# Routed adapter with LayerNorm on one core: who makes the low halves of the weights, and the order of the first tiles

## The chip, the cores and the metric

One NeuronCore of a Trainium2 chip. The metric is the device time of the kernel in microseconds. The engines are named as in the profile: PE (TensorE), DVE (VectorE), ACT (ScalarE), POOL (GpSimd), SP (SyncE, which here only issues DMAs).

## What is computed

Each of 64 batches of 64 rows of 512 numbers goes through one of three experts, chosen by an integer per batch.

```python
Wd = W_down[stream]; bd = b_down[stream]      # 512 x 256, 256
Wu = W_up[stream];   bu = b_up[stream]        # 256 x 512, 512
g = ln_w[stream];    b = ln_b[stream]
h = jnp.einsum('bsh,bhk->bsk', x, Wd) + bd[:, None, :]
h = jax.nn.gelu(h, approximate=False)
h = jnp.einsum('bsk,bkh->bsh', h, Wu) + bu[:, None, :]
h = x + h
mean = jnp.mean(h, axis=-1, keepdims=True)
var = jnp.mean(jnp.square(h - mean), axis=-1, keepdims=True)
h = (h - mean) * jax.lax.rsqrt(var + 1e-05)
return h * g[:, None, :] + b[:, None, :]
```

## The kernel before, in words

The batches are sorted by expert on the chip, so that two batches of the same expert share a tile of 128 rows; there are 33 tiles. Float32 products are made of three matmuls in a rounded format: a number is its high half (a cast on ACT) plus its low half (the difference to the cast), and a product is high by high, high by low, low by high. So each weight and each activation has a `_hi` and a `_lo` tile.

One tile t goes through these steps, each a helper in the code:

- PE `transpose_x` (L843) turns x into PSUM; ACT `x_hi` (L436) and DVE `x_lo` (L659) make its two halves; PE `down` (L850) is 12 matmuls with W_down.
- DVE `down_bias` (L665) adds the bias, ACT `gelu` (L441), PE `transpose_g` (L866), ACT `g_hi` (L446), DVE `g_lo` (L673).
- POOL `add_bias` (L358) adds x and b_up into `xb`; ACT `seed` (L451) copies that into the PSUM bank in which PE `up` (L873) then adds six matmuls with W_up.
- DVE `stats` (L679), `mean_var` (L684) and `variance` (L688); POOL `power` (L367) makes rstd; DVE `scale` (L694) makes `scaled`, ACT `rescale` (L458) makes `normed`, POOL `shift` (L373) makes `res`, which SP stores for one half of the rows and ACT for the other.

Every engine does its instructions in the order in which they are written, and waits by semaphores. In the steady loop PE does for tile t: `transpose_g(t)`, `down(t+1)`, `transpose_x(t+3)`, `up(t)`. The first tiles ("the head") are written out by hand on every engine: ACT from L488 to L535, DVE from L722 to L758, PE from L899 to L927, POOL from L384 to L399. The parts of the head that matter here:

- POOL first makes the sums of tiles 0 to 2, then the low half of W_up's second part (`w_up_low`, L255), the sum of tile 3, the low half of the third part, and then for t from 0: `shift(t-1)`, `power(t)`, `add_bias(t+4)`. DVE makes the low half of the first part, at L728.
- `rescale(t)` waits for `shift(t-2)`, because `normed` has two buffers (PAR); `scaled` has four (DEEP).
- `up(0)`, `up(1)` and `up(2)` each wait for the low half of the part of W_up that the tile needs.
- The tail of the sort (four small instructions on one partition, L653 to L657) is on DVE. It makes the places of the stores.
- SP issues the loads in the order: x0, x1, W_up part 0, x2, W_up part 1, x3, x4, W_up part 2, x5, ln_w, x6, ln_b, x7 and on.
- PE fills its waits at the start with `warm_up` matmuls on a tile of ones; `WARM_UPS` (L59) has their numbers.

## Time and profile before

| | us |
|---|---|
| median of 3 runs | 145.44 (144.79 to 146.06) |
| the profiled execution | 146.48 |
| its span | 144.3 |
| PE busy in the span | 130.2 (90%) |
| DVE busy | 111.7 (77%) |
| POOL busy | 106.4 (74%) |
| ACT busy | 85.7 (59%) |

The span is from the first to the last instruction of the program; the rest of the execution's time (2.2 us) lies around it. PEclk is the granted clock of TensorE as a share of 2.4 GHz; its lower level is half of that. PE's busy time counts matmuls; weight loads (PEld) overlap them. An entry such as "[0.82 <-POOL xb L364]" says how long the engine had been idle and what released it.

### The profile page before, as it was taken

The page shows a single profiled execution, that of the slowest core. Times are in us where ns is not written, and L with a number is a line of the kernel's source. Part 1 is how long each engine was busy: PE and PEld are TensorE (multiplying, and loading weights), DVE is VectorE, ACT ScalarE, POOL GpSimd, SP SyncE. Part 2 cuts the span into 40 slices and gives each one's busy share as a digit, 9 for nine tenths or more (in the row PEclk, how much of TensorE's full clock was granted, in tenths as well). Part 3 has the DMA queues.
Part 4 walks back from the last instruction along what each step waited for, and adds up shares of the span by engine and source line. Part 5 has one row for each costly group of instructions (what it writes and reads, how often), then busy time and mean ns, then how long its engine had stood idle before and what let it go on. Part 6 is the DMA issues. An engine that isn't in the chain of part 4 may idle for free.

```text
span 144.3 us, 4085 instructions
## 1 busy us (share of the span) xinstructions
PE 130.2 (90%) x850; PEld 116.8 (81%) x851; DVE 111.7 (77%) x275; ACT 85.7 (59%) x177; POOL 106.4 (74%) x113
## 2 busy tenths in 40 slices
PE   6899896899619999999999999999999999999840
PEld 6799795789518999999999999999999899998620
DVE  1896954869427588978897988888888888888993
ACT  1675749526446466657766666666666667666710
POOL 6000696925598388889889888998898889988961
PEclk9999999999975899999999999999999999999999
DMA  2959899844214434455444555545555653332366
GB/s 53 350 164 259 286 322 319 236 145 137 57 35 133 119 103 145 145 148 148 145 145 148 145 145 148 145 145 145 147 165 148 173 130 73 77 79 45 74 168 184
DMA packets 13200, 21.94 MB, mean 152 GB/s; under 512 B 2297, under 2 KB 3842, under 8 KB 13186
## 3 DMA queue, kind: packets, MB, share of 16 engines
q1 hardware_dynamic: 8802, 15.74, 36.1%
q10 hardware_dynamic: 4384, 6.05, 15.7%
q8 instruction: 4, 0.07, 0.2%
q14 instruction: 10, 0.08, 0.2%
HBM read 13.39 MB, written 8.65 MB: 153 GB/s over the span
## 4 chain that ended last, share of the span: by engine, by line
PE 62%; POOL 4%; DVE 3%; issue 1%; ACT 1%; POOLq 1%; ACTq 1%; DVEq 0%
PE hg_ps L861 25%; PE y_ps L894 25%; PE xT_ps L847 7%; PE hg_ps L870 4%; POOL res L381 2%; DVE res L718 1%; POOL rstd L370 1%; POOL xb L364 1%; DVE y_ps L709 1%; POOLq L208 1%; ACT normed L464 0%; DVE r_stats L682 0%; ACTq L433 0%; DVE hb L670 0%; ACT y_ps L456 0%
## 5 line engine op out<-in xcount | busy, mean ns | idle before, releaser
L381 POOL TENSOR_TENSOR res<-normed,lnb_rows 128x512 f32<-128x512 f32 x31 | 39.9, 1287 | 18.4 <-ACT normed L464 18.3
L364 POOL TENSOR_TENSOR xb<-x_sb,bu_rows 128x512 f32<-128x512 f32 x33 | 43.7, 1326 | 12.6 <-ACT bu_rows L486 12.6
L444 ACT ACTIVATE g<-hb 128x256 f32<-128x256 f32 x33 | 13.8, 418 | 35.8 <-DVE hb L670 35.7
L894 PE MATMUL y_ps<-wu_hi,gT_hi 128*128 x66 | 23.9, 444 | 6.3 <-ACT gT_hi L449 5.1
L682 DVE BATCH_NORM_STATS2 r_stats<-y_ps 128x6 f32<-128x512 f32 x33 | 23.0, 697 | 8.2 <-issue 4.4
L861 PE MATMUL hg_ps<-wd_hi,xT_hi 128*128 x132 | 24.3, 307 | 0.0
L464 ACT ACTIVATE normed<-scaled,rstd 128x512 f32<-128x512 f32 x31 | 22.4, 724 | 2.4 <-issue 2.4
L662 DVE TENSOR_TENSOR xT_lo<-xT_ps,xT_hi 128x512 fp32r<-128x512 f32 x33 | 22.7, 689 | 1.0 <-ACT xT_hi L439 1.0
L703 DVE SCALAR_TENSOR_TENSOR scaled<-y_ps,r_mv,lnw_rows 128x512 f32<-128x512 f32 x31 | 22.9, 743 | 0.0
L894 PE MATMUL y_ps<-wu_lo,gT_hi 128*128 x66 | 21.1, 402 | 0.5 <-POOL wu_lo L258 0.5
L861 PE MATMUL hg_ps<-wd_lo,xT_hi 128*128 x132 | 21.4, 285 | 0.0
L861 PE MATMUL hg_ps<-wd_hi,xT_lo 128*128 x132 | 21.3, 283 | 0.0
L894 PE MATMUL y_ps<-wu_hi,gT_lo 128*128 x66 | 21.1, 402 | 0.0
L456 ACT COPY y_ps<-xb 128x512 f32<-128x512 f32 x33 | 19.5, 590 | 2.1 <-POOL xb L364 2.0
L670 DVE TENSOR_TENSOR hb<-hg_ps,bd_rows 128x256 f32<-128x256 f32 x33 | 14.0, 423 | 7.8 <-PE hg_ps L861 7.2
L439 ACT CAST xT_hi<-xT_ps 128x512 fp32r<-128x512 f32 x33 | 18.9, 572 | 1.7 <-PE xT_ps L847 1.7
L676 DVE TENSOR_TENSOR gT_lo<-hg_ps,gT_hi 128x256 fp32r<-128x256 f32 x33 | 13.8, 418 | 7.8 <-ACT gT_hi L449 7.5
L847 PE MATMUL xT_ps<-ident,x_sb 128*128 128x128 f32 x132 | 19.6, 272 | 0.0
L370 POOL TENSOR_TENSOR rstd<-var_eps,half_neg 128x1 f32<-128x1 f32 x33 | 18.3, 553 | 1.4 <-DVE var_eps L691 1.4
L861 PEld LDWEIGHTS hg_ps<-wd_hi,xT_hi 128*128 128x128 f32 x132 | 18.3, 194 | 0.3 <-issue 0.2
L861 PEld LDWEIGHTS hg_ps<-wd_hi,xT_lo 128*128 128x128 f32 x132 | 18.3, 192 | 0.0
L861 PEld LDWEIGHTS hg_ps<-wd_lo,xT_hi 128*128 128x128 f32 x132 | 18.3, 192 | 0.0
(87 smaller groups left out, 157.0 us busy)
## 6 DMA issues: line engine op xcount, KB each, us to landing
x_sb<-in_x_dram SPq DMA_DIRECT2D x64, 128.0 KB, 2.8
out_dram<-res ACTq DMA_DIRECT2D x33, 128.0 KB, 2.4
out_dram<-res SPq DMA_DIRECT2D x33, 128.0 KB, 2.3
wd<-in_L_cond_W_down_dram ACTq DMA_DIRECT2D x3, 512.0 KB, 4.9
wu<-in_L_cond_W_up_dram SPq DMA_DIRECT2D x3, 512.0 KB, 4.8
lnw_rows<-in_L_cond_ln_w_dram SPq DMA_DIRECT2D x1, 768.0 KB, 6.3
lnb_rows<-in_L_cond_ln_b_dram SPq DMA_DIRECT2D x1, 768.0 KB, 8.0
x_sb<-in_x_dram ACTq DMA_DIRECT2D x2, 128.0 KB, 2.8
```

What stands on the lines that cost most here:

```text
L364: pool.tensor_tensor(xb[:, c % DEEP, :], x_sb[:, c % FAR, :], bu_rows[:, ds(e * H, H)], ALU.add).then_inc(xb_ready, 1)
L370: pool.tensor_tensor(rstd[:, c % DEEP:c % DEEP + 1], var_eps[:, c % DEEP:c % DEEP + 1], half_neg[:], ALU.pow).then_inc(rstd_ready, 1)
L381: pool.tensor_tensor(res[:, c % FAR, :], normed[:, c % PAR, :], lnb_rows[:, ds(e * H, H)], ALU.add).then_inc(res_ready, 1)
L439: act.copy(xT_hi[:, c % PAR, :], xT_ps[c % PAR][:]).then_inc(xhi_ready, 1)
L456: act.copy(y_ps[c % YBANKS][:], xb[:, c % DEEP, :]).then_inc(seeded, 1)
L464: act.activation(normed[:, c % PAR, :], scaled[:, c % DEEP, :], ACT.Copy, scale=rstd[:, c % DEEP:c % DEEP + 1]).then_inc(normed_ready, 1)
L662: dve.tensor_tensor(xT_lo[:, c % PAR, :], xT_ps[c % PAR][:], xT_hi[:, c % PAR, :].bitcast(F32), ALU.subtract).then_inc(xlo_ready, 1)
L682: dve.bn_stats(r_stats[:, c % DEEP, :], y_ps[c % YBANKS][:]).then_inc(stats_ready, 1)
L703: dve.scalar_tensor_tensor(out=scaled[:, c % DEEP, :], in0=y_ps[c % YBANKS][:], scalar=r_mv[:, c % DEEP, 0:1], in1=lnw_rows[:, ds(e * H, H ...
L847: mm = pe.transpose(xT_ps[c % PAR][:, k * P:(k + 1) * P], x_sb[:, c % FAR, k * P:(k + 1) * P], ident[:])
L861: mm = pe.matmul(h, x_half[:, c % PAR, k * P:(k + 1) * P], w_half[:, ds(w0 + k * BN, BN)], start=(w_half is wd_hi and x_half is xT_hi and ...
L894: mm = pe.matmul(y_ps[c % YBANKS][:], g_half[:, c % PAR, k * P:(k + 1) * P], w_half[:, ds(w0 + k * H, H)], start=False, stop=(n == 2 and k ...
```

## The change

What it does:

- DVE makes the low halves of all three parts of W_up, the first behind `down_bias(1)`, the second behind `stats(0)`, the third behind `stats(1)`. POOL makes none; it goes on with sums. `up(1)` and `up(2)` do their low-half matmuls last (high by high, low by high, high by low).
- `normed` gets four buffers: `rescale(t)` waits for `shift(t-4)`.
- The tail of the sort moves from DVE to POOL, as five small steps and a copy, each with a wait on the one before.
- POOL's head is written out: `power` and `add_bias` of three tiles come before the first `shift`.
- ACT, DVE and PE get new hand-written heads; the copies of bu into SBUF come earlier; W_up's third part is loaded before x4; one of the banks in which the down bias is spread changes; `WARM_UPS` is 10, 4, 3, 2.

```diff
-    WARM_UPS = 9, 4, 4, 2
+    WARM_UPS = 10, 4, 3, 2
-        normed = sb("normed", [P, PAR, H])
+        normed = sb("normed", [P, DEEP, H])
-        bd_banks = [y_ps[E][:], hg_ps[0][:, 0:E * BN - H]]
+        bd_banks = [y_ps[E][:], hg_ps[1][:, H - BN:H]]
...
@@ SP
             load_w_up(sp, 1, from_expert[1])
-            for t in range(3, 5):
+            load(3, 3, entries(3, 0, 2))
+            load_w_up(sp, 2, from_expert[2])
+            for t in range(4, 6):
                 load(t, t, entries(t, 0, 2))
-            load_w_up(sp, 2, from_expert[2])
-            load(5, 5, entries(5, 0, 2))
@@ POOL
-            pool.wait_ge(slots_ready, 2)
+            def mark(ins, steps):
+                ins.then_inc(marking, 1)
+                pool.wait_ge(marking, steps)
+            pool.wait_ge(rows_ready, 2)
+            pool.tensor_copy(slot_batch_f[:], slot_batch[:]).then_inc(marking, 1)
+            mark(pool.tensor_tensor(slot_step[:], key_f[:, 1:1 + SLOTS], key_f[:, 0:SLOTS], ALU.subtract), 2)
+            mark(pool.tensor_scalar(slot_same[:], slot_step[:], 0.0, float(B), ALU.is_equal, ALU.mult), 3)
+            mark(pool.tensor_tensor(slot_step[:], slot_same[:], slot_batch_f[:], ALU.add), 4)
+            mark(pool.tensor_copy(slot_store[:], slot_step[:]), 5)
+            pool.tensor_copy(io_table[:].rearrange("p (t n) -> p t n", n=3)[:, STORE_A_LAG:, 2],
+                             slot_store[:, 0:SLOTS:2]).then_inc(slots_ready, 1)
...
             for t in range(3):
                 add_bias(t, t)
-            w_up_low(pool, 1).then_inc(wu_lo_rest, 1)
             add_bias(3, 3)
-            w_up_low(pool, 2).then_inc(wu_lo_rest, 1)
+            for t in range(3):
+                power(t, t)
+                add_bias(t + DEEP, t + DEEP)
+            shift(0, 0)
+            power(3, 3)
+            shift(1, 1)
+            add_bias(3 + DEEP, 3 + DEEP)
+            power(4, 4)
+            shift(2, 2)
+            add_bias(4 + DEEP, 4 + DEEP)
+            shift(3, 3)
             def body(t, c):
-                if exists(t - 1):
-                    shift(t - 1, c - 1)
+                shift(t - 1, c - 1)
                 power(t, c)
                 add_bias(t + DEEP, c + DEEP)
-            for t in range(FAR + 1):
+            for t in range(5, FAR + 1):
                 body(t, t)
@@ ACT
-                if from_tile(t, PAR):
-                    act.wait_ge(res_ready, t - PAR + 1)
-                act.activation(normed[:, c % PAR, :], scaled[:, c % DEEP, :], ACT.Copy,
+                if from_tile(t, DEEP):
+                    act.wait_ge(res_ready, t - DEEP + 1)
+                act.activation(normed[:, c % DEEP, :], scaled[:, c % DEEP, :], ACT.Copy,
...
             wd_high(2)
+            for e in range(E - 1):
+                keep_up_bias(e)
+            x_hi(0, 0)
+            x_hi(1, 1)
             for part in range(len(bd_banks)):
                 keep_down_bias(part)
-            x_hi(0, 0)
-            keep_up_bias(0)
-            x_hi(1, 1)
-            keep_up_bias(1)
+            seed(0, 0)
             wu_high(0)
             gelu(0, 0)
-            seed(0, 0)
             g_hi(0, 0)
             x_hi(2, 2)
+            gelu(1, 1)
             wu_high(1)
-            gelu(1, 1)
+            seed(1, 1)
             g_hi(1, 1)
+            gelu(2, 2)
             x_hi(3, 3)
-            seed(1, 1)
-            gelu(2, 2)
+            wu_high(2)
+            g_hi(2, 2)
+            seed(2, 2)
+            gelu(3, 3)
             x_hi(4, 4)
-            seed(2, 2)
-            wu_high(2)
-            g_hi(2, 2)
-            gelu(3, 3)
-            x_hi(5, 5)
             seed(3, 3)
             g_hi(3, 3)
             gelu(4, 4)
+            x_hi(5, 5)
             x_hi(6, 6)
             seed(4, 4)
             rescale(0, 0)
@@ DVE
-            link(dve.tensor_copy(slot_batch_f[:], slot_batch[:]))
...
+            dve.wait_ge(up_spread, E)
+            dve.tensor_copy(bu_rows[:, (E - 1) * H:E * H], y_ps[E - 1][:]).then_inc(bu_last_ready, 1)
...
             x_lo(0, 0)
-            dve.wait_ge(up_spread, E)
-            dve.tensor_copy(bu_rows[:, (E - 1) * H:E * H], y_ps[E - 1][:]).then_inc(bu_last_ready, 1)
             x_lo(1, 1)
             dve.wait_ge(bd_ready, len(bd_banks))
             down_bias(0, 0)
-            w_up_low(dve, 0).then_inc(wu_lo_first, 1)
+            down_bias(1, 1)
+            w_up_low(dve, 0).then_inc(wu_lo_ready, 1)
             g_lo(0, 0)
-            down_bias(1, 1)
             x_lo(2, 2)
             stats(0, 0)
+            dve.wait_ge(stats_ready, 1)
+            w_up_low(dve, 1).then_inc(wu_lo_ready, 1)
+            down_bias(2, 2)
             g_lo(1, 1)
-            dve.wait_ge(stats_ready, 1)
-            down_bias(2, 2)
             mean_var(0, 0)
             variance(0, 0)
             x_lo(3, 3)
             stats(1, 1)
+            dve.wait_ge(stats_ready, 2)
+            w_up_low(dve, 2).then_inc(wu_lo_ready, 1)
             g_lo(2, 2)
-            dve.wait_ge(stats_ready, 2)
+            mean_var(1, 1)
             down_bias(3, 3)
-            mean_var(1, 1)
             variance(1, 1)
...
             x_lo(5, 5)
             scale(1, 1)
+            stats(3, 3)
+            g_lo(4, 4)
+            dve.wait_ge(stats_ready, 4)
+            down_bias(5, 5)
+            mean_var(3, 3)
+            variance(3, 3)
+            x_lo(6, 6)
             scale(2, 2)
+            scale(3, 3)
@@ PE
+                parts = [(gT_hi, wu_hi), (gT_lo, wu_hi), (gT_hi, wu_lo)] if early else [
+                    (gT_hi, wu_hi), (gT_hi, wu_lo), (gT_lo, wu_hi)]
...
-            pe.wait_ge(bd_ready, len(bd_banks))
             down(0, 0, expert_of(pe, 0))
             e0, e1 = experts_from(0)
+            pe.wait_ge(bd_ready, len(bd_banks))
             down(1, 1, e1)
             transpose_g(0, 0)
             transpose_x(2, 2)
             up(0, 0, e0)
-            transpose_x(3, 3)
...
             down(2, 2, e_down)
             transpose_g(1, 1)
-            transpose_x(4, 4)
+            transpose_x(3, 3)
             up(1, 1, e_up)
-            body(2, 2)
-            tiles(pe, body, 3, TILES - 4)
+            transpose_g(2, 2)
+            down(3, 3, e_down)
+            transpose_x(4, 4)
+            up(2, 2, e_up)
+            transpose_g(3, 3)
+            down(4, 4, e_down)
+            transpose_x(5, 5)
+            transpose_x(6, 6)
+            up(3, 3, e_up)
+            tiles(pe, body, 4, TILES - 4)
```

## Rows read from the trace of the kernel before

**Rows 1.** Page of the profile, TensorE's granted clock in 40 equal slices of the span, in tenths

```profile
PEclk9999999999975899999999999999999999999999
```

**Rows 2.** Table by stretch; columns: stretch, length, busy time (count) by engine, PEclk, DMA share, GB/s

```profile
18.00:23.40 5.40, 4.18 (x28) 3.64 (x28) 3.21 (x10) 3.24 (x7) 5.40 (x4) 1.00 0.97 328
42.60:48.60 6.00, 5.95 (x24) 5.26 (x25) 3.35 (x9) 2.37 (x5) 5.09 (x6) 0.54 0.43 133
48.60:131.80 83.20, 83.20 (x576) 75.70 (x575) 71.99 (x168) 55.83 (x120) 71.49 (x70) 1.00 0.47 133
```

**Rows 3.** Chain that ended last; columns: start us, us, engine, tile, line

```profile
39.77 0.55 POOL rstd L370
40.32 1.24 POOL xb L364
...
48.86 1.40 PE y_ps L894 x6
...
50.47 1.43 PE hg_ps L861 x12
51.90 0.44 PE xT_ps L847 x4
52.33 1.40 PE y_ps L894 x6
```

**Rows 4.** Timeline, ScalarE; columns: start us, us, engine, line, operation, tiles, [idle before]

```profile
37.13 0.59 ACT L456 COPY y_ps<-xb 128x512 f32<-128x512 f32 x1 [0.82 <-POOL xb L364]
37.66 0.72 ACT L464 ACTIVATE normed<-scaled,rstd 128x512 f32<-128x512 f32 x1
40.74 0.72 ACT L464 ACTIVATE normed<-scaled,rstd 128x512 f32<-128x512 f32 x1 [2.36 <-issue]
...
42.15 0.36 ACT L449 CAST gT_hi<-hg_ps 128x256 fp32r<-128x256 f32 x1
```

**Rows 5.** Timeline, GpSimd, in the head

```profile
15.72 1.28 POOL L364 TENSOR_TENSOR xb<-x_sb,bu_rows 128x512 f32<-128x512 f32 x1 [12.56 <-ACT bu_rows L486]
...
16.96 2.28 POOL L364 TENSOR_TENSOR xb<-x_sb,bu_rows 128x512 f32<-128x512 f32 x1
...
25.61 2.39 POOL L258 TENSOR_TENSOR wu_lo<-wu,wu_hi 128x1024 fp32r<-128x1024 f32 x1 [1.56 <-ACT wu_hi L469]
...
34.05 1.28 POOL L381 TENSOR_TENSOR res<-normed,lnb_rows 128x512 f32<-128x512 f32 x1 [4.28 <-ACT normed L464]
```

**Rows 6.** Timeline, TensorE, in the head

```profile
18.07 0.73 PE L894 MATMUL y_ps<-wu_hi,gT_hi 128*128 x2 [0.47 <-ACT gT_hi L449]
...
23.45 0.73 PE L894 MATMUL y_ps<-wu_hi,gT_hi 128*128 x2 [1.21 <-ACT y_ps L456]
...
42.65 1.22 PE L894 MATMUL y_ps<-wu_hi,gT_hi 128*128 x2 [4.10 <-ACT gT_hi L449]
...
48.61 0.71 PE L894 MATMUL y_ps<-wu_hi,gT_hi 128*128 x2
```

**Rows 7.** Timeline, VectorE, in the head

```profile
7.51 1.21 DVE L252 TENSOR_TENSOR wd_lo<-wd,wd_hi 128x1024 fp32r<-128x1024 f32 x1
...
15.85 2.24 DVE L258 TENSOR_TENSOR wu_lo<-wu,wu_hi 128x1024 fp32r<-128x1024 f32 x1
```

**Rows 8.** Page, costliest groups: busy us, mean ns of one, idle before and its releaser

```profile
L444 ACT ACTIVATE g<-hb 128x256 f32<-128x256 f32 x33 | 13.8, 418 | 35.8 <-DVE hb L670 35.7
...
L682 DVE BATCH_NORM_STATS2 r_stats<-y_ps 128x6 f32<-128x512 f32 x33 | 23.0, 697 | 8.2 <-issue 4.4
...
L662 DVE TENSOR_TENSOR xT_lo<-xT_ps,xT_hi 128x512 fp32r<-128x512 f32 x33 | 22.7, 689 | 1.0 <-ACT xT_hi L439 1.0
...
L670 DVE TENSOR_TENSOR hb<-hg_ps,bd_rows 128x256 f32<-128x256 f32 x33 | 14.0, 423 | 7.8 <-PE hg_ps L861 7.2
L439 ACT CAST xT_hi<-xT_ps 128x512 fp32r<-128x512 f32 x33 | 18.9, 572 | 1.7 <-PE xT_ps L847 1.7
```

**Rows 9.** DMA issues from 16.4 to 17.5 us; last column: us to landing

```profile
wu<-in_L_cond_W_up_dram SPq DMA_DIRECT2D x1, 512.0 KB, 5.5
```

More of the change, by code:

```diff
@@ L120, in adapter_program @@
         slot_same = sb("slot_same", [1, SLOTS])
+        slot_step = sb("slot_step", [1, SLOTS])
         slot_store = sb("slot_store", [1, SLOTS], I32)
@@ L172, in adapter_program @@
         wd_lo_ready = sem("wd_lo_ready")
-        wu_lo_first = sem("wu_lo_first")
-        wu_lo_rest = sem("wu_lo_rest")
+        wu_lo_ready = sem("wu_lo_ready")
+        rows_ready = sem("rows_ready")
+        marking = sem("marking")
         bu_last_ready = sem("bu_last_ready")
@@ L380, in shift @@
                     pool.wait_ge(stored[c % FAR], landed_count(t - FAR, c))
-                pool.tensor_tensor(res[:, c % FAR, :], normed[:, c % PAR, :], lnb_rows[:, ds(e * H, H)],
+                pool.tensor_tensor(res[:, c % FAR, :], normed[:, c % DEEP, :], lnb_rows[:, ds(e * H, H)],
                                    ALU.add).then_inc(res_ready, 1)
@@ L645, in _ @@
             w_down_low(dve, 0).then_inc(wd_lo_ready, 1)
-            dve.tensor_copy(key_f[:], key_filled[:])
-            link(dve.tensor_scalar(slot_batch[:], key_filled[:, 1:1 + SLOTS], B - 1, None, ALU.bitwise_and))
+            dve.tensor_copy(key_f[:], key_filled[:]).then_inc(rows_ready, 1)
+            dve.tensor_scalar(slot_batch[:], key_filled[:, 1:1 + SLOTS], B - 1, None, ALU.bitwise_and).then_inc(
+                rows_ready, 1)
             dve.wait_ge(wd_hi_ready, 2)
@@ L651, in _ @@
             w_down_low(dve, 2).then_inc(wd_lo_ready, 1)
-            link(dve.tensor_copy(slot_batch_f[:], slot_batch[:]))
-            link(dve.tensor_tensor(slot_same[:], key_f[:, 1:1 + SLOTS], key_f[:, 0:SLOTS], ALU.is_equal))
-            link(dve.scalar_tensor_tensor(out=slot_store[:], in0=slot_same[:], scalar=float(B), in1=slot_batch_f[:],
-                                     op0=ALU.mult, op1=ALU.add))
-            dve.tensor_copy(io_view[:, STORE_A_LAG:, 2], slot_store[:, 0:SLOTS:2]).then_inc(slots_ready, 1)
+            dve.wait_ge(up_spread, E)
+            dve.tensor_copy(bu_rows[:, (E - 1) * H:E * H], y_ps[E - 1][:]).then_inc(bu_last_ready, 1)
             def x_lo(t, c):
@@ L779, in body @@
                 return near[3], near[2]
-            for t in range(4, 6):
-                body(t, t % UNROLL)
+            body(5, 5)
             tiles(dve, body, 6, TILES - 3)
@@ L875, in up @@
                 w0 = e * (KB * H)
+                early = isinstance(t, int) and 0 < t < E
                 pe.wait_ge(ghi_ready, t + 1)
-                if isinstance(t, int) and t == 0:
-                    pe.wait_ge(wu_hi_ready, 1)
-                if isinstance(t, int) and t == 1:
-                    pe.wait_ge(wu_hi_ready, 2)
-                if isinstance(t, int) and t == 2:
-                    pe.wait_ge(wu_hi_ready, 3)
-                pe.wait_ge(seeded, t + 1)
-                for n, (g_half, w_half) in enumerate(((gT_hi, wu_hi), (gT_hi, wu_lo), (gT_lo, wu_hi))):
-                    if isinstance(t, int) and t == 0 and n == 1:
-                        pe.wait_ge(wu_lo_first, 1)
-                    if isinstance(t, int) and t == 1 and n == 1:
-                        pe.wait_ge(wu_lo_rest, 1)
-                    if isinstance(t, int) and t == 2 and n == 1:
-                        pe.wait_ge(wu_lo_rest, 2)
+                if isinstance(t, int) and t < E:
+                    pe.wait_ge(wu_hi_ready, t + 1)
+                pe.wait_ge(seeded, t + 1)
+                parts = [(gT_hi, wu_hi), (gT_lo, wu_hi), (gT_hi, wu_lo)] if early else [
+                    (gT_hi, wu_hi), (gT_hi, wu_lo), (gT_lo, wu_hi)]
+                for n, (g_half, w_half) in enumerate(parts):
+                    if w_half is wu_lo and isinstance(t, int) and t == 0:
+                        pe.wait_ge(wu_lo_ready, 1)
+                    if w_half is wu_lo and isinstance(t, int) and t == 1:
+                        pe.wait_ge(wu_lo_ready, 2)
+                    if w_half is wu_lo and isinstance(t, int) and t == 2:
+                        pe.wait_ge(wu_lo_ready, 3)
                     if g_half is gT_lo:
@@ L901, in _ @@
             transpose_x(1, 1)
-            warm_up(WARM_UPS[3], hg_ps[1])
+            warm_up(WARM_UPS[3], hg_ps[0])
             pe.wait_ge(wd_hi_ready, E)
-            pe.wait_ge(bd_ready, len(bd_banks))
             down(0, 0, expert_of(pe, 0))
             e0, e1 = experts_from(0)
+            pe.wait_ge(bd_ready, len(bd_banks))
             down(1, 1, e1)
@@ L924, in _ @@
             transpose_g(1, 1)
[L925 to L928 removed]
+            transpose_x(3, 3)
+            up(1, 1, e_up)
+            e_up, e_down = experts_from(2)
+            transpose_g(2, 2)
+            down(3, 3, e_down)
+            transpose_x(4, 4)
+            up(2, 2, e_up)
+            e_up, e_down = experts_from(3)
+            transpose_g(3, 3)
[4 more added lines that the diff above has]
+            tiles(pe, body, 4, TILES - 4)
             body(TILES - 3, TILES - 3)
```

3 lines of the change are left out of this document (1 added, 2 removed).

## The prediction, made before the changed kernel was run

> **What bounds the kernel now.** I read the page first, for the row of TensorE's granted clock: it is full in every slice but three or four, near a third of the span [rows 1]. Something stops PE once. The table by stretch then says what PE does elsewhere: from 48.6 to 131.8 us it is busy for 83.20 of 83.20 us at the full clock, while from 42.6 to 48.6 it is just as busy at 0.54 of it, and from 18.0 to 23.4 it is busy for 4.18 of 5.40 us at 1.00 [rows 2]. So the steady part is bound by PE alone and nothing on another engine can shorten it; what can be won lies before 48.6 us. In the chain of waits a steady tile is four pieces of PE: six matmuls of `up` 1.40, `transpose_g` about 0.2, `down` 1.43, `transpose_x` 0.44, and the start of `up` comes again after 52.33 - 48.86 = 3.47 us [rows 3]. I call 3.48 a tile.
>
> The same chain, just ahead of the steady part, is on POOL: a `power` of 0.55 us, then a sum of 1.24 us [rows 3]. The timeline of ACT says why that matters: `seed(5)` came after 0.82 us of idling for POOL's sum, `rescale(1)` after it, `rescale(2)` only after 2.36 us of idling, and `g_hi(5)` at 42.15 behind that and behind `seed(6)` [rows 4]. The reader should see one queue catching another: POOL idles 4.28 us in front of `shift(0)` until ACT has done `rescale(0)` [rows 5]; `power(1)`, the sum of tile 5, `shift(1)`, `power(2)` and the sum of tile 6 are all queued behind that one wait; and ACT's next steps, `g_hi(5)` among them, are queued behind these. PE has idled 4.10 us when `up(5)` begins at 42.65, and `up(6)` begins at 48.61, 5.96 us later where a tile takes 3.48: the low clock costs 2.5 us on top [rows 6]. From `up(0)` at 18.07 to `up(6)` at 48.61 it is 30.5 us for six tiles, whose work is 6 x 3.48 = 20.9. The 9.7 us between are: the stop before `up(5)` 4.1 + the low clock 2.5, the stop of 1.21 before `up(1)` [rows 6], and some 1.9 in small pieces, POOL's two late low halves of 2.39 us among them [rows 5].
>
> **The change, part by part.** The sum is made up to the start of `up(6)`, behind which PE is full either way.
>
> *POOL's head.* Three powers and the sums up to tile 6 now stand before the first `shift`. They wait for `variance` on DVE and for free buffers of `xb`, not for a `rescale`. `power(2)` needs `variance(2)`, which follows `stats(2)` after `up(2)`; by the walk below it is there at 31.0 and the sum of tile 6 at about 32.5, and ACT wants them at about 36. The cover is 3 us or more, and without it ACT would pay what is missing one for one. What is removed is the stop before `up(5)` and, if PE has no other long stop, the low clock behind it: up to 6.6 us.
>
> *Low halves.* Two POOL instructions of 2.39 us [rows 5] go and DVE gets two more. The price on DVE has two rows: 1.21 for the same shape in W_down's case, 2.24 for the first part of W_up, which ran while POOL made sums; the second of these sums took 2.28 where its neighbour took 1.28 [rows 5, 7]. So a low half costs 1.21 alone and 2.24 beside a sum, and a sum next to it 1.28 or 2.28. I take 1.21 for the first two, because POOL has no sum to do then (it has done those of tiles 0 to 2, and waits for x3 or for `variance(0)`), and 1.5 for the third, which meets the sum of tile 4. If all three cost 2.24, each puts about 1.0 us into its `up`: 3 us in all.
> The Trainium skill (SBUF — State Buffer, section "SBUF: two separate sides") says that a VectorE instruction with two SBUF inputs and a GpSimd instruction that reads SBUF exclude each other for the whole instruction, the later one waiting for the other's end. By that rule the 2.24 is 1.03 of waiting and 1.21 of work, and the price depends on where POOL is when it starts, not on being beside it; the trace agrees: 15.72 + 1.28 = 17.00, and 17.00 + 1.1 is 18.09, where the DVE instruction ended. The sum by the rule is the one with 1.21, 1.21 and 1.5; by a plain reading of the row it is the one with three times 2.24, the second rival below.
>
> *Tail of the sort.* Four instructions on one partition leave DVE at a place where it then waits for `x_hi(0)`: nothing gained. On POOL six small ones with a wait each come where it idles 12.56 us for the bias rows [rows 5]. Their inputs are there near 9.0, right behind the first W_down low half, which ends at 7.51 + 1.21 = 8.7 [rows 7]. No row shows such a step; the nearest is a `power`, 0.55 [rows 3], on 128 partitions. From below nothing, from above 0.55 and as much again for its wait, six times, 6.6 us: done between 9.0 and 15.6. I take the half, 12.3. The bias rows are then ready too, so the first sum starts near 13, before its 15.72 of now; at the upper end it starts where it does now and `up(0)` loses the 0.6 that I give it below. Value 0, range 0 to 0.6.
>
> *Walk through the head.* Durations: `gelu` 0.42, `stats` 0.70, `x_lo` 0.69, `down_bias` and `g_lo` (same size) 0.42, `x_hi` 0.57 [rows 8]; a third of `up` 0.47; a chained instruction on ACT starts 0.06 to 0.1 before the end of the one before it [rows 4]. `seed(0)` no longer stands between `transpose_g(0)` and `g_hi(0)`, which gives back its 0.59: `up(0)` starts at 17.5, not 18.07. But the low half of part 0 now stands behind `down_bias(1)`, which ends about 17.2; it ends at 18.4, so `up(0)` holds for 0.5 us after its first third and is done at 19.4. `down(2)` to 20.85, `transpose_g(1)`, `g_hi(1)`: `up(1)` at 21.6 against 23.45 [rows 6], since the 1.21 us for `seed(1)` are gone. DVE: `stats(0)` 19.65 to 20.35, low half of part 1 to 21.55, `down_bias(2)`, `g_lo(1)` to 22.4; `up(1)` holds 0.3 and ends 23.35. `down(3)` and `transpose_x(4)` take it to `up(2)` at 25.4. DVE: `stats(1)` to 24.2, low half of part 2 to 25.7, `g_lo(2)` 26.1; `up(2)` holds 0.3, ends 27.1. `down_bias(3)` ends 26.7, `gelu(3)` 27.15, `x_hi(4)` 27.65: `down(4)` starts 27.7, 0.4 us of holding. It and two `transpose_x` bring `up(3)` to 30.0, and without a stop `up(4)` comes at 33.5. Then ACT's own queue: `gelu(5)` ends about 34.3, and `x_hi(7)`, `seed(5)`, `rescale(1)`, `rescale(2)`, `seed(6)`, `g_hi(5)` stand one behind the other, 0.57 + 0.59 + 0.72 + 0.72 + 0.59 + 0.36 less six overlaps of 0.08 = 3.1 [rows 4, 8]: `up(5)` at 37.5, 0.5 after PE is free. `up(6)` at 41.0.
> So 48.61 - 41.0 = 7.6 us. The walk leaves out small delays of each release, and in such walks these only add; I take 7.4. The longest hold in it is 0.5 us, shorter than the 1.21 that left the clock at full [rows 2, 6].
>
> *Loads.* W_up's third part goes ahead of x4. It was issued at 16.5 and took 5.5 us to land, so 22.0, at a time when the DMA engines are 0.97 busy [rows 2, 9]; ahead of x4's two transfers it is there by about 21, wanted by ACT at 22.8. x4 lands later by one 512 KB transfer, 512 KB at 328 GB/s = 1.6 us [rows 2], about 21.2, wanted at 23.1 by the sum and at 24.9 by PE. Both hidden by some 2 us; the cost if that is gone is the lateness itself.
>
> *Rest.* Four buffers of `normed`: in the steady part PE is full, so nothing. One more `warm_up` at the start and one less later lie where PE waits for the sort or for x0: 0, at most 0.3 either way. The other bank for the down bias: 0. The end of the kernel keeps its order and its phase against PE: 0.
>
> Against the profiled execution: 146.48 - 7.4 = 139.1, with the 2.2 us around the span unchanged. The median of the runs shown is 1.0 below that execution; I take the same difference off it: 145.44 - 7.4 = 138.0.
>
> **The rivals.**
> 1. *The stop moves to tiles 7 to 9.* The sums of tiles 7 and 8 now stand behind `shift(1)` and `shift(2)`. ACT wants the sum of tile 9 before `g_hi(8)`, by 47.4; POOL has it, after `shift(3)`, `shift(4)` and `power(5)` at 1.28, 1.28 and 0.55 [rows 3, 5], at about 46.5. The reserve is under 1 us, and POOL is busy 71.49 of 83.20 us in the steady part [rows 2], so it catches up slowly. One tile's POOL work late is 1.28 + 0.55 + 1.24 = 3.1 us given back: 141.1; with the low clock 2.5 more, 143.6. For it: POOL was the cause before. Against: the reserve of 3 us at tiles 5 and 6.
> 2. *The shared port.* Each low half costs 2.24 and each displaced sum 2.28: 3 us of holding in `up(0)`, `up(1)`, `up(2)`, of which 0.3 is in the sum already: 138.0 + 2.7 = 140.7. For it: the one row of this kind [rows 7]. Against: POOL's idle time there.
> 3. *Slower: the clock falls in the head.* PE now holds inside `up(0)`, `up(1)`, `up(2)` and before `down(4)`, in a stretch where it is not full. If these holds bring the clock to the lower level at `up(0)`, each tile at that level costs 2.5 us more [rows 6]; it decides from three tiles on (7.5 us), and for the four up to `up(4)` the time is 138.0 + 10 = 148.0. For it: the only fall in the trace came where PE stopped, and PE's share is then below one. Against: at 4.18 busy of 5.40, with a stop of 1.21 in it, the clock stayed full [rows 2, 6], and my walk has a denser head than that.
> 4. *It does not do what it says.* `g_hi(5)` stays behind two `rescale`s and two `seed`s on ACT; if that queue and not POOL's was what held `up(5)`, only the small stops go, 1.5 to 2.5 us: 143.4. Against: ACT idled 0.82 and 2.36 us within it [rows 4].
>
> **How the numbers follow.** Forecast 0.66, rival 1 0.14, rival 2 0.09, rival 3 0.04, rival 4 0.07. The forecast's own range is 136.8 to 139.6: the walk's holds are 2.0 us in all, of which a half could be absent, and a sort's tail or a load could cost 0.5 to 1.5. Downward the end is PE without any hold, 7.4 + 2.0 = 9.4 saved, 136.0. For 8 in 10 I take half of rivals 1 and 2 in: 136.6 to 141.1. A difference under about 1% can't be told from none here, that is 1.45 us. Faster by over 1% (below 143.99): forecast, rivals 1 and 2 and most of 4, 0.92; within 1%: 0.04; slower: 0.04.
>
> **What would show it.** Right: PEclk full in all slices behind the start; `up(5)` with under 1.5 us of idle time before it; `up(6)` at 40.5 to 42; the two L258 instructions near 1.2 us and the third up to 2.4; no wait of POOL for `normed` in front of a sum before tile 7; the stretch from `up(6)` to the end as long as before. Wrong: a second dip of PEclk; ACT idling before `seed(8)` or `seed(9)` (rival 1); all three low halves at 2.2 (rival 2); PE idling before `up(5)` with ACT busy all through (rival 4).

## The result, and the profile after

The changed kernel takes 139.2 us in the median (138.98 to 139.67, 4 runs) against 145.22 for the kernel before on the same chip (144.79 to 146.06, 4 runs). The ratio is 0.9583, with a 95% interval of 0.9531 to 0.9634: 6.0 us less. The profiled execution took 139.21 us with a span of 137.2, against 146.48 and 144.3. A run more than 1.5% above the fastest of its kernel is left out of the ratios.

The page, PE's busy time and the granted clock in 40 slices:

```profile
PE 126.6 (92%) x850; PEld 112.5 (82%) x851; DVE 112.9 (82%) x273; ACT 85.1 (62%) x177; POOL 104.5 (76%) x117
...
PEclk9999999999999999999999999999999999999995
```

The dip of [rows 1] near a third of the span is gone, and PE is busy for 126.6 us where it was for 130.2: the same matmuls, none of them at the low clock behind a stop. The table by stretch, to lay beside [rows 2] (columns as there):

```profile
18.00:23.40 5.40, 5.29 (x30) 3.84 (x29) 4.58 (x10) 3.54 (x8) 1.92 (x3) 1.00 1.05 270
41.00:124.00 83.00, 83.00 (x574) 75.64 (x573) 71.81 (x169) 55.35 (x120) 73.02 (x72) 1.00 0.48 137
```

From 18.0 to 23.4 us PE is busy for 5.29 us instead of 4.18, and from 41 us on it is full, as it was from 48.6. The timeline of PE, the first matmuls of each `up` (and the second third of `up(0)`); the columns are start, duration, engine, line, operation, tiles, and in brackets the idle time before and who ended it:

```profile
17.51 0.73 PE L923 MATMUL y_ps<-wu_hi,gT_hi 128*128 x2
18.24 0.70 PE L923 MATMUL y_ps<-wu_lo,gT_hi 128*128 x2
...
21.85 0.73 PE L923 MATMUL y_ps<-wu_hi,gT_hi 128*128 x2
...
25.50 0.71 PE L923 MATMUL y_ps<-wu_hi,gT_hi 128*128 x2
...
29.85 0.71 PE L923 MATMUL y_ps<-wu_hi,gT_hi 128*128 x2
...
33.41 0.71 PE L923 MATMUL y_ps<-wu_hi,gT_hi 128*128 x2
...
37.74 0.73 PE L923 MATMUL y_ps<-wu_hi,gT_hi 128*128 x2 [0.60 <-ACT gT_hi L473]
...
41.23 0.71 PE L923 MATMUL y_ps<-wu_hi,gT_hi 128*128 x2
```

`up(5)` waits 0.60 us for `g_hi(5)` where it waited 4.10 [rows 6], and `up(6)` starts at 41.23 instead of 48.61. That is 7.4 us; the span is 7.1 us shorter, so the rest is 0.3 us longer. PE is full up to 124 us; about half of the 0.3 us is spread over the tiles (23 of them take 80.04 us, 79.89 before), the other half lies in the last tiles, where PE is no longer full. Its cause was not followed. ACT in front of `up(5)`, to lay beside [rows 4]:

```profile
34.96 0.59 ACT L480 COPY y_ps<-xb 128x512 f32<-128x512 f32 x1
35.48 1.34 ACT L488 ACTIVATE normed<-scaled,rstd 128x512 f32<-128x512 f32 x2
...
36.72 0.58 ACT L480 COPY y_ps<-xb 128x512 f32<-128x512 f32 x1
37.23 0.37 ACT L473 CAST gT_hi<-hg_ps 128x256 fp32r<-128x256 f32 x1
```

`seed(5)`, both rescales and `seed(6)` run one behind the other with no idle time between, where ACT had waited 0.82 and 2.36 us for POOL. (The view names "issue" for the 2.36; the last thing that `rescale(2)` needs is POOL's `power(2)`, which ended at 39.77 + 0.55 = 40.32 [rows 3], 0.42 us before it.) POOL in the head:

```profile
8.75 0.23 POOL L365 CAST slot_batch_f<-slot_batch 1x66 f32<-1x66 int32 x1 [5.60 <-DVE slot_batch L671]
8.96 1.26 POOL L366 TENSOR_TENSOR slot_step<-key_f 1x66 f32<-1x66 f32 x1
10.30 1.43 POOL L367 TENSOR_SCALAR slot_same<-slot_step 1x66 f32<-1x66 f32 x1
...
13.26 3.77 POOL L379 TENSOR_TENSOR xb<-x_sb,bu_rows 128x512 f32<-128x512 f32 x3 [0.54 <-issue]
19.38 1.29 POOL L379 TENSOR_TENSOR xb<-x_sb,bu_rows 128x512 f32<-128x512 f32 x1 [2.34 <-DMA x_sb<-in_x_dram]
...
33.09 1.28 POOL L396 TENSOR_TENSOR res<-normed,lnb_rows 128x512 f32<-128x512 f32 x1 [0.63 <-ACT normed L488]
```

Its first sum starts at 13.26 instead of 15.72, the three behind each other take 3.77 us with none stretched, and `shift(0)` at 33.09 waits for the same `normed` as before [rows 5], but nothing that ACT wants soon stands behind it. The first three lines of the fence are small steps of the sort, and two of them take 1.26 and 1.43 us on one partition; that comes back below. DVE's three low halves of W_up, to lay beside [rows 7]:

```profile
16.19 1.93 DVE L260 TENSOR_TENSOR wu_lo<-wu,wu_hi 128x1024 fp32r<-128x1024 f32 x1
...
20.18 1.56 DVE L260 TENSOR_TENSOR wu_lo<-wu,wu_hi 128x1024 fp32r<-128x1024 f32 x1
...
24.49 1.23 DVE L260 TENSOR_TENSOR wu_lo<-wu,wu_hi 128x1024 fp32r<-128x1024 f32 x1
```

### The profile page after: what moved, and what is told of

Read it like the earlier page. It is cut to its first block, busy times and chain, and to the rows that moved or that the text cites. A ratio compares the mean times of both kernels' runs of the same rounds, so it can differ in the third digit from the quotient of the medians.

```text
span 137.2 us, 4086 instructions
## 1 busy us (share of the span) xinstructions
PE 126.6 (92%) x850; PEld 112.5 (82%) x851; DVE 112.9 (82%) x273; ACT 85.1 (62%) x177; POOL 104.5 (76%) x117
## 4 chain that ended last, share of the span: by engine, by line
PE 70%; DVE 11%; POOL 6%; ACT 5%; issue 3%; DMA 2%; POOLq 1%; ACTq 1%; DVEq 0%
PE hg_ps L891 28%; PE y_ps L923 28%; PE xT_ps L877 8%; PE hg_ps L900 5%; POOL res L396 2%; DMA itok_all_i<-in_itok_B_dram 2%; DVE r_stats L704 1%; ACT xT_hi L463 1%; DVE hb L692 1%; ACT y_ps L480 1%; DVE res L740 1%; DVE scaled L725 1%; POOL slot_same L367 1%; POOL slot_step L366 1%; POOLq L210 1%
## 5 line engine op out<-in xcount | busy, mean ns | idle before, releaser
L379 POOL TENSOR_TENSOR xb<-x_sb,bu_rows 128x512 f32<-128x512 f32 x33 | 42.7, 1296 | 2.9 <-DMA x_sb<-in_x_dram 2.3
L923 PE MATMUL y_ps<-wu_hi,gT_hi 128*128 x66 | 23.3, 434 | 1.4 <-ACT gT_hi L473 1.2
L385 POOL TENSOR_TENSOR rstd<-var_eps,half_neg 128x1 f32<-128x1 f32 x33 | 18.2, 551 | 7.9 <-DVE var_eps L713 7.8
L923 PE MATMUL y_ps<-wu_lo,gT_hi 128*128 x66 | 20.6, 393 | 0.0
L877 PEld LDWEIGHTS xT_ps<-ident,x_sb 128*128 128x128 f32 x132 | 15.1, 140 | 0.8 <-DMA x_sb<-in_x_dram 0.5
```

What stands on the lines that cost most here:

```text
L379: pool.tensor_tensor(xb[:, c % DEEP, :], x_sb[:, c % FAR, :], bu_rows[:, ds(e * H, H)], ALU.add).then_inc(xb_ready, 1)
L385: pool.tensor_tensor(rstd[:, c % DEEP:c % DEEP + 1], var_eps[:, c % DEEP:c % DEEP + 1], half_neg[:], ALU.pow).then_inc(rstd_ready, 1)
L877: mm = pe.transpose(xT_ps[c % PAR][:, k * P:(k + 1) * P], x_sb[:, c % FAR, k * P:(k + 1) * P], ident[:])
L923: mm = pe.matmul(y_ps[c % YBANKS][:], g_half[:, c % PAR, k * P:(k + 1) * P], w_half[:, ds(w0 + k * H, H)], start=False, stop=(n == 2 and k ...
```

## The experiments

Two theories stood against each other. A: what cost the time was the order on POOL alone, a shift that waits with sums queued behind it. B: what cost it was POOL's load, the two low halves of 2.39 us [rows 5], with ACT's queue behind it. The kernel before ran beside every group of runs; its median was 145.76, 146.19, 145.56 and 144.95 us in the four groups, so kernels of different groups are compared by their ratios to it.

The record has the span of every run too. The device time lies 2.0 to 2.1 us above it in most runs, 1.7 to 1.8 in e4 and e5, and in some runs of several kernels 2.4 to 3.5; why is not known. With four runs of a kernel this can move a median by more than an edit does, so spans are given below where the two disagree. The changed kernel's are 136.9 to 137.6 us.

### One part alone, and that part taken out

`e1_sums_first` is the kernel before with one edit, `e2_shifts_first` the changed kernel with that edit undone.

```diff
-            def body(t, c):
-                if exists(t - 1):
-                    shift(t - 1, c - 1)
+            for t in range(3):
+                power(t, t)
+                add_bias(t + DEEP, t + DEEP)
+            shift(0, 0)
+            power(3, 3)
+            shift(1, 1)
+            add_bias(3 + DEEP, 3 + DEEP)
...
```

> The kernel before, with one edit: POOL's head in the new order (power and sum of tiles 0 to 2 ahead of the first shift). The low halves of W_up's parts 1 and 2 stay on POOL, the heads of ACT, DVE and PE stay as they were. Theory A (the shift that waits for rescale(0) holds up the sums queued behind it, and that is the stop before up(5)): the stop of 4.1 us shrinks to under 1 us, no low clock behind it, up(6) starts near 42.3 instead of 48.61, and the time is 139 to 140.5. Theory B (POOL is late because it also makes two low halves, and ACT's queue does the rest): the stop stays above 2.5 us and the time above 142.5.

> The changed kernel, with POOL's head put back into the old order (shift(t-1), power(t), sum t+4 from the start) and everything else of the change kept, the low halves on DVE and four buffers of normed among it. Theory A: the stop before up(5) is back with 4 us or more, with the low clock behind it, up(6) near 47.6, time 144.5 to 146: the rest of the change is worth almost nothing without the order. Theory B: POOL has no low halves any more, so the stop is under 2 us and the time 139.5 to 142.

e1: 139.7 us (139.25 to 140.23), ratio 0.9593 (0.9527 to 0.9659). e2: 145.73 us (144.43 to 146.96), ratio 1.0013 (0.9964 to 1.0062). PE's timeline of e1 at `up(5)` and `up(6)`:

```profile
39.05 0.72 PE L905 MATMUL y_ps<-wu_hi,gT_hi 128*128 x2 [0.45 <-ACT gT_hi L460]
...
42.54 0.71 PE L905 MATMUL y_ps<-wu_hi,gT_hi 128*128 x2
```

And of e2 the table by stretch, the stop before `up(5)` at 41.45 and what follows it:

```profile
41.00:46.50 5.50, 5.05 (x24) 4.50 (x25) 3.42 (x9) 2.69 (x7) 5.14 (x6) 0.69 0.49 143
36.90:41.45 4.55, 0.00 (x0) 0.00 (x1) 0.10 (x1) 1.89 (x4) 4.01 (x4) 1.00 0.22 59
```

With the order alone the stop is 0.45 us and `up(6)` starts at 42.54, where 42.3 was expected. Without it, all the rest of the change is worth nothing: PE does nothing at all for 4.55 us, and then works at 0.69 of its clock. Both halves of theory A hold. In e2 PE reaches the stop 1.7 us earlier than in the kernel before (`up(4)` starts at 33.17 against 34.83), and only stands longer for the same release.

### Who makes the low halves

`e3_lows_on_pool` is the changed kernel with the low halves of parts 1 and 2 back on POOL.

```diff
             for t in range(3):
                 add_bias(t, t)
+            w_up_low(pool, 1).then_inc(wu_lo_rest, 1)
             add_bias(3, 3)
+            w_up_low(pool, 2).then_inc(wu_lo_rest, 1)
...
-            w_up_low(dve, 1).then_inc(wu_lo_ready, 1)
-            w_up_low(dve, 2).then_inc(wu_lo_ready, 1)
```

> The changed kernel, with the low halves of parts 1 and 2 back on POOL at their old places (behind the sum of tile 2 and behind the sum of tile 3), the order of the rest kept. Theory A: no large stop; up(1) and up(2) wait for a low half of 2.39 us, which costs 0.5 to 1.5 us: 139.7 to 140.7. Theory B: the low halves are what made POOL late; the stop before up(5) returns with 2 us or more and the time is above 142.

138.82 us (138.68 to 139.63), ratio 0.9561 (0.9491 to 0.9631): below the 139.7 to 140.7 that my theory gave, and level with the changed kernel or a little below it (spans 136.6 to 136.8 us against 136.9 to 137.6). Theory B falls; so does my cost for the move.

```profile
17.58 0.73 PE L924 MATMUL y_ps<-wu_hi,gT_hi 128*128 x2
...
37.07 0.72 PE L924 MATMUL y_ps<-wu_hi,gT_hi 128*128 x2 [0.35 <-ACT gT_hi L476]
...
40.57 0.71 PE L924 MATMUL y_ps<-wu_hi,gT_hi 128*128 x2
```

From `up(0)` to `up(6)` it is 22.99 us here and 23.72 in the changed kernel. The likely reason, read from the queues and not tested apart: on DVE each low half stands in front of `down_bias` and `g_lo`, for which ACT and PE wait; on POOL, with the sums ahead, it stands in front of nothing that is wanted soon. The part of the change that its title names first gains nothing, and in this place may cost some tenths.

### The stop and the low clock, apart

`e4_stop_filled` and `e5_stop_filled` are the kernel before with PE kept at work during the stop, so that the clock stays. The first try:

```diff
+            pe.wait_ge(xlo_ready, 8)
+            warm_up(14, xT_ps[1])
             up(5, 5, e_up)
```

> The kernel before, with 14 warm_up matmuls on a bank that is free then, put before up(5), where PE stood still for 4.1 us; nothing is left out of the computation. It takes the low clock away and leaves the stop. If the low clock costs what the spacing of up(5) and up(6) says (2.5 us), up(6) starts 2.5 us earlier and the median is 142.5 to 143. Rival: the low clock costs the median nothing or under 1 us, since the runs of before that are not profiled may not have it: 144.3 or more.

150.23 us (148.82 to 150.59), ratio 1.0294 (1.0209 to 1.0380). PE's timeline:

```profile
44.97 4.84 PE L807 MATMUL xT_ps<-ones 128*128 128x128 f32 x28 [5.69 <-DVE xT_lo L663]
49.56 0.71 PE L895 MATMUL y_ps<-wu_hi,gT_hi 128*128 x2
```

I had overlooked that DVE makes `x_lo(7)` behind `g_lo(5)`, which waits for the same `g_hi(5)` as `up(5)`: the fill could only start when the stop was over, and ran in front of `up(5)`, its first 3 us at the low clock. It says nothing on the question. The second try uses the PSUM bank of tiles 3 and 7:

```diff
+            pe.wait_ge(scaled_ready, 4)
+            for _ in range(14):
+                mm = pe.matmul(y_ps[3][:, 0:P], ones[:], ones[:], start=False, stop=True, skip_group_check=True)
+            mm.then_inc(filled, 1)
             up(5, 5, e_up)
```

> The kernel before, with 14 matmuls on the ones tile put before up(5), on the PSUM bank of tiles 3 and 7, which is free from the end of scale(3) (seed(7) waits for the last of them); PE can start them where it stood still for 4.1 us. Nothing is left out of the computation. The stop stays, the low clock behind it goes: up(6) starts 3.5 us after up(5), the mean granted clock is 0.99 or more. If the low clock costs what the profiled execution shows (2.5 us), the median is 142.5 to 143.3. Rival: that execution had more of it than the others (mean clock 0.974; other executions of before have 0.973 to 0.986), and the median falls by only 1 to 2 us, 143.7 to 144.7.

143.33 us (143.21 to 143.64), ratio 0.9826 (0.9755 to 0.9897), mean granted clock 0.992 to 0.997.

```profile
38.09 3.29 PE L939 MATMUL y_ps<-ones 128*128 128x128 f32 x28
42.39 0.73 PE L898 MATMUL y_ps<-wu_hi,gT_hi 128*128 x2 [1.00 <-ACT gT_hi L451]
...
45.92 0.71 PE L898 MATMUL y_ps<-wu_hi,gT_hi 128*128 x2
```

`up(5)` starts at 42.39, where it was 42.65 before [rows 6], and `up(6)` 3.53 us behind it, where it took 5.96. So the low clock is worth 1.5 to 3.6 us by the ratio's interval, 2.5 in the middle; a gain there is beyond the noise, but whether it exceeds 2% is open. Of these 2.5 us some 0.3 lie outside the span (1.74 us there instead of 2.03). The order alone (e1) saves 5.9 us, so some 3.4 are left for the stop itself, which fits the 3.65 us by which it shrank (4.10 to 0.45). And the runs draw together: 0.4 us between the lowest and the highest, where the kernel before went from 144.76 to 146.42 in the six runs of the same group that the ratio uses. In the first group its thirteen runs have mean clocks of 0.973 to 0.986; at 0.975 and below their spans are 143.4 to 144.5 us, above that 142.5 to 143.4: how long the clock stays low differs from run to run. Two traces show it: in the kernel before it is at the lower level from about 41.3 to 48.1 us, in e2 from about 42.2 to 45.6, and `up(6)` follows `up(5)` by 5.96 and by 5.05 us.

### Two buffers of `normed`, and the sort's tail

`e7_two_normed` is the changed kernel with PAR for DEEP in `normed` and in the wait of `rescale`.

> The changed kernel, with two buffers of normed instead of four (rescale(t) waits for shift(t-2)). Theory: with the sums ahead of the shifts, each shift is done 1.5 us or more before the rescale that would wait for it (shift(0) ends at 34.4, rescale(2) starts at 36.1; shift(1) ends at 37.7, rescale(3) starts at 39.2), so nothing changes: 139.0 to 139.5, up(5) within 0.2 us of 37.74. Rival: two buffers bring the stop back in part, up(5) 1 us or more later, 140 or above.

139.32 us (139.06 to 140.23), ratio 0.9575 (0.9495 to 0.9655), `up(5)` at 37.53. The four buffers do nothing once the sums stand ahead.

`e6_tail_on_dve` is the changed kernel with the four instructions of the sort's tail back on DVE.

```diff
+            link(dve.tensor_copy(slot_batch_f[:], slot_batch[:]))
+            link(dve.tensor_tensor(slot_same[:], key_f[:, 1:1 + SLOTS], key_f[:, 0:SLOTS], ALU.is_equal))
...
             dve.wait_ge(up_spread, E)
```

> The changed kernel, with the four small instructions of the sort's tail back on DVE behind the third low half of W_down, and none on POOL. Theory: DVE copies the last bias rows about 0.9 us later, POOL's first sum starts at 13.9 to 14.2 instead of 13.26, seed(0), the first part's high half and gelu(0) follow by 0.5 us, up(0) starts near 18.0 instead of 17.51: 139.4 to 139.9. Rival: POOL's small steps of 1.26 and 1.43 us beside DVE's low halves go as well, nothing that PE waits for moves, 138.9 to 139.3.

139.68 us (139.53 to 140.43), ratio 0.9593 (0.9517 to 0.9670), `up(0)` at 17.94. `up(0)` is 0.43 us later, as the theory had it. The spans are 137.5 to 137.8 us against 136.9 to 137.6 of the changed kernel, and 137.0 to 137.5 of e7 beside it, so some 0.4 us; by the ratios it would be 0.15 us only, and their intervals overlap.

### The last hold, and what the rest of the head is worth

`e8_g_hi_first` is the changed kernel with this in ACT's head, and `body(6)` without its first two steps:

```diff
             seed(5, 5)
+            g_hi(5, 5)
             rescale(1, 1)
             rescale(2, 2)
+            seed(6, 6)
```

> The changed kernel, with g_hi(5) put ahead of rescale(1), rescale(2) and seed(6) in ACT's queue. Theory: the last hold in the head, 0.6 to 0.8 us before up(5) at 37.74, is ACT's own queue of 3.1 us behind gelu(5); it goes, up(5) starts near 36.95, up(6) near 40.4, and the time is 138.4 to 138.8. Rival: the rescales and the seed that are put back make tg(6) or up(6) late by as much, 139.0 to 139.5.

139.31 us (138.94 to 139.37), ratio 0.9555 (0.9486 to 0.9624).

```profile
17.96 0.73 PE L926 MATMUL y_ps<-wu_hi,gT_hi 128*128 x2
...
37.15 0.70 PE L926 MATMUL y_ps<-wu_hi,gT_hi 128*128 x2
...
40.62 0.70 PE L926 MATMUL y_ps<-wu_hi,gT_hi 128*128 x2
```

The hold before `up(5)` is gone: `up(0)` to `up(6)` is 22.66 us instead of 23.72. But `up(0)` itself came 0.45 us later than in the profile of the changed kernel, and the median stayed. The median hides the gain, though: the spans of the four runs are 136.9, 136.4, 136.4 and 136.6 us, against 136.9 to 137.6, some 0.6 us less, as the theory had it; the device times of the last three lie 2.7 to 3.0 us above their spans, those of the changed kernel 2.0 to 2.1. The rival, that something behind is late by as much, falls: `up(6)` follows `up(5)` by 3.47 us, and only `up(8)` comes 0.2 us late (3.68 behind `up(7)`). The profiled execution has the longest span of the four, and the question became what moves `up(0)`.

`e9_both` joins e3 and e8.

> The changed kernel with two edits: the low halves of W_up's parts 1 and 2 back on POOL (as in e3_lows_on_pool) and g_hi(5) ahead of the rescales (as in e8_g_hi_first). Theory: the low halves cost DVE more of the path than they cost POOL (up(6) came 22.99 us after up(0) in e3, 23.72 in the changed kernel), and the hold of 0.35 us before up(5) that was left in e3 goes too: up(6) 22.6 us after up(0), median 138.2 to 138.7, below the changed kernel and e3. Rival: POOL is late with two low halves, power(0) and the sums behind them hold up seed(5) or seed(6), and it is 138.9 or more.

138.59 us (138.27 to 139.36), ratio 0.9546 (0.9499 to 0.9594), `up(0)` at 17.94 and `up(6)` at 40.30, 22.36 us apart. The theory's number, with spans of 135.7 to 136.5 us.

### The port between DVE and POOL

`e10_sum_waits` is the changed kernel with one wait more on POOL.

```diff
-            for t in range(3):
+            for t in range(2):
                 add_bias(t, t)
+            pool.wait_ge(wu_lo_ready, 1)
+            add_bias(2, 2)
```

> The changed kernel; POOL's sum of tile 2 waits for DVE's first low half of W_up. Theory (exclusion: an instruction of DVE with two SBUF inputs waits for the end of the sum under way, and then works 1.09 us): the first low half takes 1.1 to 1.25 us instead of 1.93 and ends at 17.4, up(0) goes through without a hold of 0.25 us, and no sum is slowed; 138.8 to 139.2. Rival (the two share a port and slow each other in proportion, or the low half is slow for another reason, loads into SBUF for one): it still takes 1.6 us or more.

140.01 us (139.59 to 140.29), ratio 0.9638 (0.9577 to 0.9698). DVE's first low half of W_up:

```profile
16.87 1.22 DVE L260 TENSOR_TENSOR wu_lo<-wu,wu_hi 128x1024 fp32r<-128x1024 f32 x1 [0.50 <-ACT wu_hi L495]
```

It takes 1.22 us instead of 1.93, as exclusion has it, and `up(0)` goes through without a hold. The low half itself ended at 18.09, not at the 17.4 expected, because the high half that it needs came late. In the changed kernel the sum of tile 2 runs from 15.77 for 1.27 us, to 17.04, and the low half ends at 16.19 + 1.93 = 18.12, 1.08 us later; the next one ends at 21.74, 1.07 us behind the sum of tile 3 (19.38 + 1.29 = 20.67). The kernel was slower all the same, by 0.8 us of its ratio. For the profiled execution, whose span of 137.8 us is 0.6 above that of the changed kernel, POOL's timeline shows why:

```profile
9.33 2.30 POOL L365 CAST slot_batch_f<-slot_batch 1x66 f32<-1x66 int32 x1 [6.17 <-DVE slot_batch L673]
11.60 0.29 POOL L366 TENSOR_TENSOR slot_step<-key_f 1x66 f32<-1x66 f32 x1
```

The first of the sort's small steps, 0.23 us in the changed kernel's profile, takes 2.30 here. The data for it came at 9.3 us, just after DVE had begun two low halves of W_down one behind the other, 2.34 us from 9.19; the step ends when they end. In e9 it takes 1.17. POOL's first sum then starts at 13.96 instead of 13.26, and `seed(0)`, the high half of W_up's first part, `gelu(0)` and `up(0)` follow on ACT's queue in that order. So whether `up(0)` comes at 17.5 or at 18.2 hangs on a few tenths of a us near 9 us. The edit does not touch that stretch, so this delay is chance and not its price. The other three runs have spans of 137.0, 137.1 and 137.5 us, like the changed kernel's, and two of them carry 3.0 and 3.3 us outside the span: the edit has no clear cost or gain in the spans.

### Versions that are faster

`e11_low_first` is e9 with two pairs exchanged:

```diff
@@ ACT
-            seed(0, 0)
             wu_high(0)
+            seed(0, 0)
             gelu(0, 0)
@@ DVE
-            down_bias(1, 1)
             w_up_low(dve, 0).then_inc(wu_lo_ready, 1)
+            down_bias(1, 1)
```

> As e9_both, with the first low half of W_up ahead of down_bias(1) on DVE and the first high half ahead of seed(0) on ACT. Theory: the low half is there before up(0) needs it, so up(0)'s second third follows its first without the 0.25 us of holding, and down_bias(1) has 0.7 us to spare before gelu(1): 0.2 to 0.3 us below e9_both. Rival: the low half meets a sum there too, down_bias(1) and gelu(1) come late and up(1) with them, 0.3 us or more above e9_both.

137.67 us (137.25 to 138.97), ratio 0.9484 (0.9429 to 0.9539), 0.9 us below e9, more than the 0.2 to 0.3 expected. In e9 ACT waited for POOL's first sum, then made `seed(0)`, the high half of 1.04 us and `gelu(0)` (at 16.49); here it makes the high half while it would wait, from 13.93, and `gelu(0)` starts at 15.57:

```profile
17.02 0.73 PE L927 MATMUL y_ps<-wu_hi,gT_hi 128*128 x2
...
35.90 0.70 PE L927 MATMUL y_ps<-wu_hi,gT_hi 128*128 x2
...
39.37 0.70 PE L927 MATMUL y_ps<-wu_hi,gT_hi 128*128 x2
```

The low half did meet a sum, as the rival had it (2.31 us from 15.02), and `up(1)` still came 4.33 us behind `up(0)`; the time lost there was less than the time won.

`e12_tail_later` is e11 with the sort's tail moved on POOL:

```diff
-            pool.wait_ge(rows_ready, 2)
-            pool.tensor_copy(slot_batch_f[:], slot_batch[:]).then_inc(marking, 1)
...
-            for t in range(3):
+            for t in range(2):
                 power(t, t)
                 add_bias(t + DEEP, t + DEEP)
+            pool.wait_ge(rows_ready, 2)
+            pool.tensor_copy(slot_batch_f[:], slot_batch[:]).then_inc(marking, 1)
...
```

> As e11_low_first, with the six small steps of the sort's tail on POOL moved from ahead of its first sum to behind the sum of tile 5, where POOL idles some 2 us for variance(2). Theory: near 9 us these steps meet DVE's low halves of W_down, and the first of them takes 0.23 us or, where it comes just after a low half has begun, 1.17 (e9, e11) or 2.30 (e10); that sets when the first sum starts (13.26 to 13.96). Moved, each takes 0.45 or less, the first sum starts at 13.0 or before, the first low half of W_up ends earlier by the same, and the median is 137.1 to 137.6. Rival: the first sum has to wait for the bias rows until 13.5 anyway, or the moved steps hold up power(2), and the median is 137.7 or more.

137.19 us (137.12 to 138.44), ratio 0.9472 (0.9422 to 0.9521). POOL's timeline, the first sums and the first three moved steps, and PE's:

```profile
12.90 4.76 POOL L373 TENSOR_TENSOR xb<-x_sb,bu_rows 128x512 f32<-128x512 f32 x3 [9.74 <-DVE bu_rows L689]
...
28.50 0.23 POOL L405 CAST slot_batch_f<-slot_batch 1x66 f32<-1x66 int32 x1
28.69 0.29 POOL L406 TENSOR_TENSOR slot_step<-key_f 1x66 f32<-1x66 f32 x1
29.06 0.46 POOL L407 TENSOR_SCALAR slot_same<-slot_step 1x66 f32<-1x66 f32 x1
```

```profile
17.03 0.72 PE L931 MATMUL y_ps<-wu_hi,gT_hi 128*128 x2
...
38.90 0.71 PE L931 MATMUL y_ps<-wu_hi,gT_hi 128*128 x2
```

The first sum starts at 12.90, and beside no low half the steps take 0.23, 0.29 and 0.46 us. `up(6)` starts at 38.90, 2.3 us ahead of the changed kernel. This is the best version: 5.3% below the kernel before, where the change gives 4.2%. Against e11 it is a small step: spans of 135.1 to 135.3 us after 135.2 to 135.9, with ratios whose intervals overlap. The head still has 21.87 us for six tiles of 3.48.

## Why the prediction was right, and where it was off

**What bounds it, and the stop.** Right. PE is full behind the head in both kernels, the gain is the distance of the two `up(6)`, and the cause was the wait of `shift(0)` with the sums queued behind it: e1 has the gain with the order alone, e2 has none without it.

**The walk.** `up(0)` to `up(6)` were given as 17.5, 21.6, 25.4, 30.0, 33.5, 37.5 and 41.0; they came at 17.51, 21.85, 25.50, 29.85, 33.41, 37.74 and 41.23. ACT's queue behind `gelu(5)` was the last hold, 0.60 us for the 0.5 given, and e8 takes it away. Part of this closeness is luck: `up(0)` came at 17.51 here, but at 17.96 in e8 and 17.94 in e9, which are the same up to that point, and the first low half ended near the 18.4 of the walk (18.12) for another reason than the walk gave.

**Low halves.** The step that took 1.21 us for the first two, "because POOL has no sum to do then", was wrong: they took 1.93 and 1.56. DVE began the first at 16.19, not at 17.2, while the three sums, one behind the other from 13.26, ran until 17.04; and the sum of tile 3, which had waited 2.34 us for x3, ran until 20.67. The third, given 1.5, took 1.23. The second rival's 2.24 each was wrong as well: the price is what is left of the sum under way, and then 1.08. The Trainium skill's rule (SBUF — State Buffer, section "SBUF: two separate sides"), by which the later of the two waits for the end of the other's instruction, is borne out by these ends and by the 1.22 us of e10. What I did not see is that the move has no use at all: e3 is as fast without it.

**The sort's tail.** Given as done at 12.3 with a value of 0: it was done at 12.72. The value was 0.4 us (e6), on the side of a gain that I had excluded with the words "nothing gained"; DVE copies the last bias rows 0.9 us earlier, and in e6 POOL's first sum, and through it `up(0)`, waits for them. In the changed kernel the rows are there at 12.01, and the first sum (13.26) stands behind POOL's own last step of the sort (to 12.72) instead: e12, with the steps out of the way, has it at 12.90. That the small steps would meet DVE's low halves was not in my bounds by its cause; the upper bound of 6.6 us covered it.

**Loads, buffers, banks.** The loads stayed hidden behind ACT and PE: PE waits 0.4 us in all for x, before its first tiles. POOL waits 2.34 us for x3, for a sum that ACT wants only at 27.27. Four buffers: nothing, as given (e7).

**From the profile to the median.** This is the term that was mis-sized. The forecast for the profiled execution was 139.1 us, and it took 139.21. I then took 1.0 us off, because the profiled execution of before lay that far above its median, and gave 138.0 for the median, which was 139.2. The distance was not a constant of profiled executions. Most of it belongs to the stop: that execution had a mean clock of 0.974, at the long end of what the low clock lasts, and in the first group of runs of the kernel before those at 0.975 and below have a median span of 143.95 us, the others of 142.8, which is 1.1 us less. With the stop filled (e5) the runs lie within 0.4 us. The clocks of the four runs behind the 145.22 are not on record; that its median had less of the low clock is inferred. What the change removes was thus 7.3 us in the profiled execution and 6.0 in the median, and of the 1.2 us between 138.0 and 139.2 this is 1.0.

**The rivals.** No stop at tiles 7 to 9: POOL has the sum of tile 9 at 46.4, and PE is full. No fall of the clock in the head, where the longest hold is 0.83 us, before `transpose_g(0)`. The fourth had the queue right and the size wrong: PE does idle before `up(5)` with ACT busy all through, its sign, but for 0.60 us, and the stop of 4.10 went with POOL's order.

## What to carry to other kernels

In an engine's queue, put what others wait for ahead of what waits for others: one `shift` that waited 4.3 us, with two sums behind it that ACT wanted, was worth more than all else that this change did. Before you move work to another engine, undo the move in an otherwise finished version; here it bought nothing, and the engine that took it had the tighter queue. When a kernel has a stop that lets the clock fall, its runs scatter, and a single profiled execution overstates or understates the gain by as much as they scatter. And look at the spans beside the device times: for e8 and e10 the medians alone said the wrong thing about edits worth some tenths.
